# Computing a cross network's sums in four quarters of TensorE instead of in one block-diagonal matmul per pair of samples

## The reference

```
x: (512, 39, 64), W0: (39, 39, 128), W1: (39, 128, 128)
h1 = einsum('bid,bjd,ijh->bhd', x, x,  W0)
h2 = einsum('bid,bjd,ijh->bhd', x, h1, W1)
out = concatenate([h1, h2], axis=1).sum(axis=-1)      # (512, 256)
```

## Time and profile before

| | us |
|---|---|
| median of 3 runs | 420.26 (419.84 to 421.49) |
| the profiled execution, its own time | 420.18 |
| its span, first to last instruction | 418.4 |
| TensorE matmuls busy | 405.7 (97%) |
| TensorE loads busy | 390.0 (93%) |
| VectorE busy | 152.9 (37%) |
| ScalarE busy | 121.9 (29%) |

### The profile page before, as it was taken

How to read it: one execution, slowest core, us unless ns; L and a number is a source line. 1 busy time by engine, 2 the same in 40 slices (tenths; PEclk the granted TensorE clock), 3 DMA queues, 4 the chain that set the end, 5 groups by cost and what they waited for, 6 DMA issues and landing times.

```text
span 418.4 us, 7831 instructions
## 1 busy us (share of the span) xinstructions
PE 405.7 (97%) x3640; PEld 390.0 (93%) x3640; DVE 152.9 (37%) x180; ACT 121.9 (29%) x250; POOL 9.2 (2%) x10
## 2 busy tenths in 40 slices
PE   0999999999999999999999999999999999999997
PEld 0666899999999999999999999999999999999996
DVE  3017498000770734252424514261536070702000
ACT  1466433334422320413042314131421322132300
POOL 8000000000000000000000000000000000000000
PEclk9999999999999999999999999999999999999999
DMA  8902430000300017000000350000005000000000
GB/s 312 334 21 59 193 125 3 2 2 0 127 2 2 2 40 202 12 2 14 0 2 2 73 181 0 15 2 2 0 2 127 2 1 14 2 2 2 0 2 13
DMA packets 4336, 19.77 MB, mean 47 GB/s; under 512 B 592, under 2 KB 1104, under 8 KB 3920
## 3 DMA queue, kind: packets, MB, share of 16 engines
q1 hardware_dynamic: 3728, 18.75, 13.9%
q10 hardware_dynamic: 576, 0.52, 0.4%
HBM read 18.75 MB, written 0.52 MB: 46 GB/s over the span
## 4 chain that ended last, share of the span: by engine, by line
PE 97%; DMA 1%; DVE 1%; SPq 0%; ACT 0%; issue 0%
PE stage L445 46%; PE out_ps L477 30%; PE stage L410 7%; PE stage L430 6%; PE stage L428 6%; PE stage L413 2%; DMA arena<-in_w_rows 1%; DVE arena L246 1%; DVE arena L248 0%; SPq L214 0%; ACT arena L373 0%
## 5 line engine op out<-in xcount | busy, mean ns | idle before, releaser
L445 PE MATMUL stage<-arena 128*110 128x80 f32 (+2 forms) x2048 | 195.4, 258 | 0.0
L445 PEld LDWEIGHTS stage<-arena 128*110 128x110 f32 (+2 forms) x2048 | 194.7, 174 | 0.0
L382 ACT COPY arena<-stage 110x480 f32<-110x480 f32 (+5 forms) x176 | 79.7, 453 | 194.1 <-PE stage L445 194.1
L477 PE MATMUL out_ps<-arena 110*128 110x128 f32 (+3 forms) x968 | 127.8, 293 | 0.0
L477 PEld LDWEIGHTS out_ps<-arena 110*128 110x128 f32 (+2 forms) x968 | 121.8, 192 | 4.1
L308 DVE TENSOR_TENSOR arena<-arena 128x3200 f32<-128x3200 f32 x16 | 55.8, 3489 | 73.3 <-PE stage L445 73.2
L430 PE MATMUL stage<-arena 128*110 128x128 f32 (+1 forms) x234 | 44.7, 273 | 0.0
L428 PE MATMUL stage<-arena 128*110 128x128 f32 (+1 forms) x234 | 44.7, 273 | 0.0
L410 PE MATMUL stage<-arena 128*128 128x380 f32 (+1 forms) x78 | 34.5, 525 | 10.2 <-DVE arena L248 10.2
L311 DVE TENSOR_TENSOR arena<-arena 128x640 f32<-128x640 f32 x16 | 13.2, 826 | 68.6 <-PE stage L445 68.6
L430 PEld LDWEIGHTS stage<-arena 128*110 128x110 f32 (+1 forms) x234 | 32.9, 172 | 0.0
(11 more groups left out here) (20 smaller groups left out, 33.9 us busy)
## 6 DMA issues: line engine op xcount, KB each, us to landing
arena<-in_x_dense SPq DMA_DIRECT2D x8, 640.0 KB, 6.5
arena<-in_x_single SPq DMA_DIRECT2D x16, 320.0 KB, 4.7
arena<-in_c_first SPq DMA_DIRECT2D x1, 2560.0 KB, 9.3
arena<-in_w SPq DMA_DIRECT2D x2, 640.0 KB, 7.2
arena<-in_c_second SPq DMA_DIRECT2D x1, 1280.0 KB, 5.7
arena<-in_w SPq DMA_DIRECT2D x1, 1216.0 KB, 9.8
arena<-in_w_square SPq DMA_DIRECT2D x1, 800.0 KB, 4.6
arena<-in_c_one SPq DMA_DIRECT2D x2, 256.0 KB, 9.9
```

Source lines behind the costliest of these rows:

```text
L382: nc.scalar.copy(view((s_x0 if tile % 2 else s_w0) + 2 * t, (B, count), (1, 2 * some), rows=(0, rows)), banks[g % RING][0:rows, FIRST[tile ...
L445: done = nc.tensor.matmul(bank[:, 2 * (t - t0):2 * (t - t0) + 2, :], view(prod0[(2 * p + hf) % PRODS] + in_unit * W_ROWS, (1, rows)), view ...
L477: done = nc.tensor.matmul(to, sums, w, start=tile == 0 and s == 0, stop=tile == TILES - 1 and s == COUNT[tile] - 1, skip_group_check=True)
```

## The change

The sums of a pair are made by four matmul calls instead of one. Each sample of the pair has its own 64 partitions, as before, but its own matmuls, and its products are cut in two parts: 60 and 50 (tiles of 110), 50 and 50 (tile of 100), 50 and 59 (tile of 109). The first part's results go to PSUM partitions 0 onward, the second part's to partitions 64 onward. So the four calls use the four combinations of a lower or upper half of the partitions read and a lower or upper half of the partitions written. Each sample has a PSUM bank of its own, so banks are claimed in twos. The moving operand is now the sample's own third fields: 40 of them, or the 20 or 21 that are wanted. A bank holds 12 samples (40 fields) or 24 (20 or 21 fields).

Since the second part now begins at partition 64, the tiles of sums have a gap of unused partitions and span 114, 114, 114 and 123 partitions. The mixed weights, the rows of W0 and the vectors for the first layer are laid out with the same gap; GpSimd zeroes the gap (four more small fills), the long addition at line 261 is cut in two, and the loads of W0's rows grow from 840 to 912 words a partition. Samples lie in the tiles of sums with all first members of the pairs ahead of all second ones, so the output is stored by two DMAs of 64 partitions with a stride, instead of one. The weighing is the same but for the number of partitions, and stays in one block behind each pass's sums.

```diff
+PART = 64
+W_FIRST = 60
+X_FIRST = 50
+W_SPAN = PART + W_ROWS - W_FIRST
+X_SPAN = PART + X_ROWS - X_FIRST
...
+        FIRST_PART = [W_FIRST, X_FIRST, W_FIRST, X_FIRST]
+        SPAN = [PART + r - f for r, f in zip(ROWS, FIRST_PART)]
...
-        GROUP = [6, 6, 6, 6]
+        GROUP = [12, 24, 12, 24]
...
-                act.dma_start(out[n * B:(n + 1) * B, :], view(out_sb0, (1, 2 * HID))).then_inc(out_stored, 16)
+                samples = out[n * B:(n + 1) * B, :].rearrange("(t of) h -> of t h", of=2)
+                for of in range(2):
+                    act.dma_start(samples[of], view(out_sb0, (1, 2 * HID), rows=(of * PAIRS, (of + 1) * PAIRS)))\
+                        .then_inc(out_stored, 16)
...
                 for t, some in groups(tile):
-                    act.wait_ge(filled, g + 1)
-                    nc.scalar.copy(view((s_x0 if tile % 2 else s_w0) + 2 * t, (B, count), (1, 2 * some), rows=(0, rows)),
-                                   banks[g % RING][0:rows, FIRST[tile] * 2 * some:(FIRST[tile] + count) * 2 * some]
-                                   .rearrange("p (s b) -> p s b", b=2 * some))\
-                        .then_inc(emptied, 1)
-                    g += 1
+                    for of in range(2):
+                        act.wait_ge(filled, g + 2 - of)
+                        nc.scalar.copy(view((s_x0 if tile % 2 else s_w0) + of * PAIRS + t, (B, count), (1, some),
+                                            rows=(0, rows)),
+                                       banks[g % RING][0:rows, 0:count * some].rearrange("p (s b) -> p s b", b=some))\
+                            .then_inc(emptied, 1)
+                        g += 1
...
+            def sum_pair(p, t, g):
...
+                if t == t0:
+                    claim(g)
+                    claim(g + 1)
+                if in_unit == 0:
+                    if tile == 0:
+                        pe.wait_ge(single_loaded[hf], 32 * (p // TILES + 1))
+                    pe.wait_ge(prod_ready, 2 * p + hf + 1)
+                for of in range(2):
+                    on = (of * P // 2, (of + 1) * P // 2)
+                    for part, (r0, r1) in enumerate([(0, FIRST_PART[tile]), (FIRST_PART[tile], rows)]):
                         done = nc.tensor.matmul(
-                            bank[:, 2 * (t - t0):2 * (t - t0) + 2, :],
-                            view(prod0[(2 * p + hf) % PRODS] + in_unit * W_ROWS, (1, rows)),
-                            view(single0 + t * SLOTS, (PAIRS * SLOTS, 2), (1, SLOTS)), start=True, stop=True)
+                            banks[(g + of) % RING][PART * part:PART * part + r1 - r0, 0:count * some]
+                            .rearrange("p (i b) -> p b i", b=some)[:, t - t0, :],
+                            view(prod0[(2 * p + hf) % PRODS] + in_unit * W_ROWS + r0, (1, r1 - r0), rows=on),
+                            view(single0 + (of * PAIRS + t) * SLOTS + first, (1, count), rows=on), start=True, stop=True)
+                if t < t0 + some - 1:
+                    return g
+                done.then_inc(filled, 2)
+                return g + 2
```

More of the change, by code:

```diff
@@ L47, in x_pairs, with place @@
     return [(base + a, base + QUARTER + c) for a in range(QUARTER) for c in range(QUARTER)]
+def place(row, first):
+    return row if row < first else PART + row - first
 def cin_kernel(nc: bass.Bass, x_dense: bass.AP, x_single: bass.AP, w0_square: bass.AP, w0_rows: bass.AP,
@@ L172, in banks_through @@
         def banks_through(p):
-            counts = [len(groups(t)) for t in range(TILES)]
+            counts = [2 * len(groups(t)) for t in range(TILES)]
             return SETUP_BANKS + (p + 1) // TILES * sum(counts) + sum(counts[:(p + 1) % TILES])
@@ L353, in _ @@
                     act.wait_ge(filled, g + 1)
-                    rows = X_ROWS if kind == "x" else W_ROWS
+                    rows = X_SPAN if kind == "x" else W_SPAN
                     field = first_field(half, kind) + i
@@ L482, in _ @@
-            g = sum_pass(0, g)
-            for p in range(1, PASSES):
-                g = sum_pass(p, g)
-                weigh_pass(p - 1)
-            weigh_pass(PASSES - 1)
+                rows, count, first = ROWS[tile], COUNT[tile], FIRST[tile]
+                hf, in_unit = divmod(t, HALF_PAIRS)
+                t0 = t // GROUP[tile] * GROUP[tile]
+                some = min(GROUP[tile], PAIRS - t0)
+                if t == t0:
+                    claim(g)
+                    claim(g + 1)
@@ new lines, in sum_pair, with weigh @@
+                if t < t0 + some - 1:
+                    return g
+                done.then_inc(filled, 2)
+                return g + 2
+            def weigh(p, s):
+                n, tile = divmod(p, TILES)
+                rows = SPAN[tile]
+                if s == 0:
+                    pe.wait_ge(emptied, banks_through(p))
+                    if tile == 0:
+                        if n == 0:
+                            pe.wait_ge(one_ready, 1)
+                        else:
+                            pe.wait_ge(out_copied, n)
+                    if p == 3:
+                        pe.wait_ge(c1_ready, 1)
+                    if p < TILES:
+                        pe.wait_ge(emptied, SETUP_BANKS)
+                sums = view((s_x0 if tile % 2 else s_w0) + s * B, (1, B), rows=(0, rows))
+                if s == (0 if tile == 1 else 20):
+                    w, to = view(one_c0 + tile * HID, (1, HID), rows=(0, rows)), out_ps[:, 0:HID]
+                elif tile == 3:
+                    w, to = view(c_xb0 + 2 * HID * s, (1, 2 * HID), rows=(0, rows)), out_ps[:, 0:2 * HID]
+                else:
+                    c0 = c_xa0 if tile == 1 else c_w0[tile // 2]
+                    w, to = view(c0 + s * HID, (1, HID), rows=(0, rows)), out_ps[:, HID:2 * HID]
+                last = tile == TILES - 1 and s == COUNT[tile] - 1
+                done = nc.tensor.matmul(to, sums, w, start=tile == 0 and s == 0, stop=last, skip_group_check=True)
+                if last:
+                    done.then_inc(batch_done, 1)
@@ L507 @@
                 continue
-            tile, row = (2 * half, r) if r < W_ROWS else (2 * half + 1, r - W_ROWS)
+            is_x = r >= W_ROWS
+            row = place(r - W_ROWS, X_FIRST) if is_x else place(r, W_FIRST)
+            tile, r = 2 * half + is_x, row + W_SPAN * is_x
             rows[0, :, half, r] = one[0, row, tile] = w0[f, g]
```

127 lines of the change are left out of this document (54 added, 73 removed).

## The result

The changed kernel takes 465.25 us in the median of four runs (460.85 to 467.63); the kernel before, on the same chip, 420.54 (419.84 to 421.49). The ratio is 1.105, with a 95% interval from 1.095 to 1.115. The forecast was 436.1 us. The direction was right, but the loss is 44.7 us and not 16, and most of it stands where the prediction saw nothing. Where one of the two runs of an experiment was over 1.5% slower than the other (experiments 5 and 8), the faster one is compared and the other stands in brackets.

The account below looks back on a forecast made before the run. The prediction took the kernel to be bound by TensorE's starts, paced by loads in the sums. 420.2 + 10.6 (sums) + 4.9 (borders) + 0.4 (setup, end) = 436.1 us; forecast's own range 425 to 450, overall range 335 to 650 us.

Parts of the forecast that it names:

- What bounds the kernel before: Whole kernel: TensorE's starts set the time, their distance being the larger of load and matmul; TensorE busy 97%.
- two loads at a time: Sums: each call costs one load's time instead of two, so the sums take 203.6 us, +10.6 us.
- one load runs ahead: TensorE's loads: one load runs ahead of the matmuls and no more, read from the start of the kernel.
- Rival A: Sums: all four quarters work at once, 110.0 ns a pair with tiles of 110; 340.5 us in all, chance 0.28.
- Rival C, the issue of instructions: Sums: distance between instructions sets the time, anywhere up to 955 us, 642 us in its middle; chance 0.13.
- 4.7 ns each, no limit by itself: Instruction code fetched by DMA: 1.2 us a 16 KB packet, 64 bytes an instruction, so 4.7 ns each.
- no chance of its own: TensorE's granted clock falling to 1.2 GHz where less of the array works: given no chance, as it stayed at 1.00.
- Borders, +4.9 us: 30 changes between quarter and whole array, at most 163 or 164 ns each; upper end of 0 to 5 us taken.
- Setup and end, +0.4: W0's longer rows at the very start +0.2 us; a second store issue at the end +0.2 us.
- rival B: Sums: one load at a time, everything in turn, 214.2 us more; 639.7 us in all, chance 0.24.

Follow-up runs that it names:

- experiment 5: experiment 4 with each moving operand streamed twice and 6 or 12 samples in a bank: 470.62 us, its slower run 479.61.
- experiment 8: experiment 3 with two more small matmul calls a pair, so 16 instructions a pair: 771.19 us with one column, 456.84 us (slower run 464.37) with 33.
- experiment 3: Changed kernel with column halves: both samples in one matmul on 128 partitions, products in two parts, two calls a pair: 355.65 and 356.32 us, ratio 0.846.
- experiment 4: Changed kernel with row halves: samples apart on 64 partitions, products in one part, two calls a pair: 583.60 us, ratio 1.388.
- experiment 7: experiment 3 with each weighing cut into four pieces, one behind every 16 pairs: 369.56 us, ratio 0.878.
- experiment 1: Changed kernel with each weighing cut into four pieces between the next pass's sums, same instructions in another order: 398.71 us, ratio 0.948.
- experiment 6: Changed kernel with its moving operands streamed twice, six or twelve samples in a bank: 446.82 us, ratio 1.063.
- experiment 2: Changed kernel with each weighing cut into 32 pieces, one behind every two pairs: 528.74 us, ratio 1.257.

## Why the prediction was wrong

- **What bounds the kernel before**: right. TensorE's starts set everything; VectorE, ScalarE, banks and SyncE's loads stayed under cover, and TensorE waited for none of them.
- **Sums, "two loads at a time", +10.6 us**: the step that failed. It took "one load runs ahead", read from loads of the whole array, as a rule for loads of different quarters. Measured: 13.0 ns a couple, four at once, where the forecast needs 203.6 us / 8192 = 25. With that alone the sums would have taken 107 us; they took 214.2, 21.2 more than before, because of the two steps that follow. Rival A's price (110 ns a pair) was right for the array, as the Trainium skill, TensorEngine Tiling (Array Packing), Key Properties, has it that different tiles work in parallel; experiments 3 and 4 show it for either direction alone.
- **Rival C, the issue of instructions**: its form was right, its threshold too (over 12.4 ns an instruction the forecast's sums are passed), but it had 0.13, most of it above 600 us. The false sentence is "4.7 ns each, no limit by itself": it divided the time for which a packet was in flight by its instructions, though one packet does not follow on the other at once. Measured, a packet of 256 instructions comes every 3.5 to 4.0 us, 14 to 16 ns an instruction, though its own transfer takes 0.9 to 1.5. At 15 ns 16384 of them would be 246 us; the sums took 214, because the first 107 to 241 couples of a block needed no new packet. The Trainium skill, TensorEngine Tiling (Array Packing), Instruction Overhead, gives each matmul some 60 cycles of overhead; couples that start 13.0 ns apart in different quarters do not show such a floor between them.
- **The clock, "no chance of its own"**: wrong. I had concluded from blocks of whole-array work that it would hold. The weighing took 24.0 us more than before; with column halves at full clock it took 2.2 more, so about 22 us are the clock's. In the sums, too, 2224 of the 8192 couples ran at half clock.
- **Borders, +4.9 us**: right as far as shown; 30 x 147 ns = 4.4 us, a price measured between halves and the whole array (experiment 7), not between quarters and the whole.
- **Setup and end, +0.4**: too low. The second store cost more than the 0.2 us given for it. Its view is below; one took 0.34 us, and from the last matmul to the end of the span it is 3.43 us for 2.56, in every version with two stores. The sums begin at 98.3 us for 97.4, but that start varies from 97.2 to 98.6 us between the versions, so it can't be put down to the change.

```profile
462.39 1.12 ACTq L403 DMA_DIRECT2D out<-arena  x2
```

The time fell between the forecast and rival B because a gain of 86 us in array work (193 to 107) was more than eaten: from start to start, 80 us of waits for instructions, 27 us more than 107 in the couples themselves, most of it at half clock, and 24 us in the weighing. That the direction came out right is no merit of the step.

The packets' times in the trace and experiments 1, 3 and 6 settle that the instructions' arrival sets the sums' time: fewer of them, or the same spread out, or more work in each, all make the kernel faster, and the pieces start some 2.4 us after a packet does. What remains open is why packets come 3.5 to 4.0 us apart when the transfer of one takes 0.9 to 1.5; no run varied their size or the load on the DMA engines. Why the clock fell where TensorE had no gap (experiments 2 and 4) is open too.

## What to carry to other kernels

Before cutting a matmul into parts that use a quarter of the array, divide the block's time by its instructions: at under 15 ns each over more than about 500 instructions TensorE starves here, however well the parts overlap (the short blocks of experiment 3, 512 instructions in 6.14 us, came through). Take the split that gives the overlap with the fewest instructions (column halves have half as many as quarters and are 15% faster than the kernel before), try more columns streaming for each load (it gained 113 and 18 us in experiments 5 and 6), and lay long instructions next to dense short ones. Price a change of arrangement at 0.15 us, as measured between halves and the whole array.

## What the hardware did that I had not expected

- TensorE's clock fell to half while it was busy without a gap (experiment 4: 99% busy, mean 0.65), and came back when the same loads had twice as many columns streamed behind them (experiment 5, blocks of 110). The Trainium skill, TensorE: Matmul & The Clock Gate, Part 1, says that the gate follows how busy the PE has been; the changed kernel agrees in that its clock fell in blocks with gaps, and experiments 2 and 4 show it falling where the profile has next to none.
- Streaming useless columns made two kernels faster: 583.6 to 470.6 us and 465.3 to 446.8 us.
- Instruction code is a resource of its own: 13.0 ns a couple inside a packet, 30 ns a couple over packets (3.8 us / 128).
